# An expert layer's low weight parts move from VectorE to GpSimd, and accumulations are waited for by slot

## The reference

```python
xt = x.reshape(B * S, d)                                  # 4096 x 256
scores = jax.nn.softmax(xt @ router_w, axis=-1)
expert_weights, expert_idx = jax.lax.top_k(scores, 2)
h = gelu(jnp.einsum('td,edf->tef', xt, w1)) * jnp.einsum('td,edf->tef', xt, v1)   # F = 704
y = jnp.einsum('tef,efd->ted', h, w2)
yk = jnp.take_along_axis(y, expert_idx[:, :, None], axis=1)
out = jnp.sum(expert_weights[:, :, None] * yk, axis=1) + bias
```

## Time and profile before

| | before |
|---|---|
| time, median of 3 runs | 918.5 us (917.31 to 919.8) |
| the profiled execution's own time | 916.48 us |
| its span | 914.7 us |
| expert stage | from about 403 us to the end |
| PE busy | 823.5 us, 90% of the span |
| DVE busy | 578.7 us, 63% |
| POOL busy | 445.7 us, 49% |
| ACT busy | 370.3 us, 40% |

### The profile page before, as it was taken

How to read it: one execution, slowest core, us unless ns; L and a number is a source line. 1 busy time by engine, 2 the same in 40 slices (tenths; PEclk the granted TensorE clock), 3 DMA queues, 4 the chain that set the end, 5 groups by cost and what they waited for, 6 DMA issues and landing times.

```text
span 914.7 us, 19914 instructions
## 1 busy us (share of the span) xinstructions
PE 823.5 (90%) x5017; PEld 730.6 (80%) x5018; DVE 578.7 (63%) x1636; ACT 370.3 (40%) x672; POOL 445.7 (49%) x444
## 2 busy tenths in 40 slices
PE   6799999999999985019999999999999999999994
PEld 2588898898989874018998988989989898999993
DVE  6668777888758565504666565566665756655553
ACT  4775666657474332103233242342432434232221
POOL 1344655968668685822345344343343533433433
PEclk9799999999999986559999999999999999999998
DMA  7111050211302314362224224242252222222221
GB/s 266 36 47 47 2 167 24 94 63 55 93 3 94 95 34 147 128 219 55 46 35 132 47 35 132 45 132 36 38 141 35 35 43 39 35 39 42 35 47 17
DMA packets 49207, 65.31 MB, mean 71 GB/s; under 512 B 4944, under 2 KB 43984, under 8 KB 49168
## 3 DMA queue, kind: packets, MB, share of 16 engines
q1 hardware_dynamic: 35200, 46.03, 17.5%
q0 software_dynamic: 13392, 18.27, 9.9%
q10 hardware_dynamic: 576, 0.54, 0.2%
HBM read 41.28 MB, written 23.54 MB: 71 GB/s over the span
## 4 chain that ended last, share of the span: by engine, by line
PE 83%; POOL 5%; DMA 3%; DVE 3%; issue 2%; ACT 2%; SPq 1%; DVEq 0%; ACTq 0%; POOLq 0%
PE ps L1379 13%; PE ps L1381 13%; PE ps L1380 13%; PE ps L466 10%; PE ps L468 10%; PE ps L467 10%; PE ps L1412 5%; DMA out_rows<-y_moe,tok_moe 2%; POOL routed L1248 2%; PE ps L1388 2%; PE ps L558 1%; PE ps L1427 1%; PE ps L1426 1%; POOL w_moe_lo L371 1%; PE ps L515 1%
## 5 line engine op out<-in xcount | busy, mean ns | idle before, releaser
L1565 POOL TENSOR_TENSOR y_moe<-y_moe 128x256 f32<-128x256 f32 x71 | 51.9, 731 | 245.1 <-DVE y_moe L1529 245.1
L1379 PE MATMUL ps<-w_moe_hi,xT_moe_hi 128*128 x426 | 167.4, 393 | 1.4 <-DVE xT_moe_lo L1511 1.4
L1381 PE MATMUL ps<-w_moe_lo,xT_moe_hi 128*128 x426 | 161.4, 379 | 0.0
L1380 PE MATMUL ps<-w_moe_hi,xT_moe_lo 128*128 x426 | 161.1, 378 | 0.0
L1571 POOL DMA_INDIRECT out_rows<-y_moe,tok_moe x71 | 111.2, 1566 | 33.9 <-issue 33.4
L1470 ACT ACTIVATE hidT_hi<-ps 128x768 fp32r<-128x768 f32 x71 | 57.9, 815 | 163.8 <-PE ps L1412 163.8
L1464 ACT ACTIVATE gelu_moe<-ps 128x704 f32<-128x704 f32 x71 | 54.0, 760 | 133.8 <-PE ps L1381 133.8
L1379 PE MATMUL ps<-w_moe_hi,hidT_hi 128*128 x355 | 105.8, 298 | 2.3 <-issue 2.3
L1381 PE MATMUL ps<-w_moe_lo,hidT_hi 128*128 x355 | 100.3, 283 | 0.0
L1380 PE MATMUL ps<-w_moe_hi,hidT_lo 128*128 x355 | 99.9, 281 | 0.0
L1529 DVE SCALAR_TENSOR_TENSOR y_moe<-ps,gate_moe,gates 128x256 f32<-128x256 f32 x142 | 62.1, 479 | 51.8 <-PE ps L1427 45.8
(11 more groups left out here) (195 smaller groups left out, 1973.5 us busy)
## 6 DMA issues: line engine op xcount, KB each, us to landing
raw<-in_w SPq DMA_DIRECT2D x8, 1408.0 KB
x_moe<-routed SPq DMA_DIRECT2D x74, 132.5 KB, 2.2
raw<-in_w SPq DMA_DIRECT2D x8, 640.0 KB
x_sb<-in_x SPq DMA_DIRECT2D x8, 512.0 KB, 3.7
x_again<-in_x SPq DMA_DIRECT2D x8, 512.0 KB
out_rows<-x_again SPq DMA_DIRECT2D x8, 512.0 KB
gu_raw<-in_gu_t SPq DMA_DIRECT2D x1, 1536.0 KB, 7.3
out_rows<-y_moe,tok_moe POOLq DMA_INDIRECT x71, 4.2
```

Of the source, the lines that this page charges most:

```text
L1379: pe.matmul(dst, a_hi, b_hi, start=first, stop=False)
L1380: pe.matmul(dst, a_lo, b_hi, start=False, stop=False)
L1381: return pe.matmul(dst, a_hi, b_lo, start=False, stop=last)
```

## The change

The low parts of the first layer's weights are made on POOL instead of DVE: at an expert change POOL makes three pieces in a row (128x1408 twice, 128x1536 once) ahead of the accumulation of the tile. DVE's step has no split and no table entry for it. The two waits for `added` on DVE are set by the four slots: in step t, `take_gates` of tile t+1 waits for tile t-3, and `gate_y` of tile t-1 for tile t-5. Seven tiles instead of three are written out ahead of the loop, since the loop's body may now only hold tiles with t >= 4 for these waits; SP's loads keep their distances.

```diff
--- before.py
+++ after.py
@@ -1316,7 +1316,7 @@
             def near(self, d):
                 return Tile(self.n + d, self.turn)
 
-        ALONE = 3
+        ALONE = 7
 
         def tiles(engine, first, step, last):
 
@@ -1365,11 +1365,13 @@
                 load_rows(Tile(n))
                 if n == 1:
                     load_weights(sp, 2, 3, 1)
+                if n >= SLOTS + 2:
+                    load_behind(Tile(n - SLOTS - 1))
 
             with sp.Fori(0, (MOE_TILES - ALONE) // SLOTS, 1) as turn:
                 for n in range(SLOTS):
                     load_rows(Tile(n + SLOTS + ALONE - 1, turn))
-                    load_behind(Tile(n + 1, turn))
+                    load_behind(Tile(n + ALONE - 2, turn))
             for n in range(SLOTS):
                 sp.wait_ge(rows_in[n], ((MOE_TILES + SLOTS - 2 - n) // SLOTS + 1) * 16)
 
@@ -1502,8 +1504,8 @@
                 v.tensor_tensor(g[:, 2:3], g[:, 0:1], g[:, 1:2], ALU.mult).then_inc(gate_steps, 1)
                 v.wait_ge(gate_steps, t.v * 2 + 2)
                 v.tensor_tensor(g[:, 3:4], g[:, 0:1], g[:, 2:3], ALU.subtract)
-                if t.n >= ALONE:
-                    v.wait_ge(added, (t.v - ALONE + 1) * 16)
+                if t.n >= SLOTS:
+                    v.wait_ge(added, (t.v - SLOTS + 1) * 16)
                 v.tensor_copy(tok_moe[:, t.slot, :], tok).then_inc(gates_r, 1)
 
             def xT_rest(t):
@@ -1523,8 +1525,8 @@
             def gate_y(t):
                 v.wait_ge(y_mm, t.v + 1)
                 v.wait_ge(gates_r, t.v + 1)
-                if t.n >= 2:
-                    v.wait_ge(added, (t.v - 1) * 16)
+                if t.n >= SLOTS:
+                    v.wait_ge(added, (t.v - SLOTS + 1) * 16)
                 for b in range(B):
                     i = v.scalar_tensor_tensor(y_moe[:, t.slot, b, :], y_ps[t.par], gate_moe[:, t.slot, 3 - b:4 - b],
                                                gates[:, b, 1, :], ALU.mult, ALU.mult)
@@ -1547,18 +1549,21 @@
                 take_gates(t.near(1))
 
             def step(t):
-                e = to_be_split(v, t)
                 multiply(t)
                 xT_rest(t.near(1))
                 gate_y(t.near(-1))
                 hidT_rest(t)
                 take_gates(t.near(1))
-                split_behind(v, e, t, split_w13_lo)
 
             tiles(v, first, step, gate_y)
 
         @block.gpsimd
         def _(g):
+            def split_lo(g, e, buf, t):
+                g.wait_ge(we_hi, 3)
+                split_w13_lo(g, e, buf)
+                split_w2_lo(g, e, buf)
+
             def add_rows(t):
 
                 g.wait_ge(y_r, t.v + 1)
@@ -1574,7 +1579,7 @@
 
             def step(t):
                 e = to_be_split(g, t)
-                split_behind(g, e, t, split_w2_lo)
+                split_behind(g, e, t, split_lo)
                 add_rows(t)
 
             tiles(g, add_rows, step, lambda t: None)
```

## The result

The changed kernel takes 943.66 us (median of 4 runs, 942.32 to 946.25) against 919.15 for the kernel before in the same series: a ratio of 1.027, with an interval of 1.025 to 1.029. The change makes the kernel slower by 24.5 us. The direction was forecast, the size was not: the forecast was 922.7 with 918 to 928 around it. The profiled execution after took 943.01 us and spans 941.2; before, it was 916.48 and 914.7.

A forecast was written before the change was run, and what follows sets the result against it. PE bounds the kernel, with gaps worth 9.3 us, mostly waits for DVE's `hid_moe` at six expert changes. Gaps of 13.5 after against 9.3 give +4.2: 920.6 on the profiled 916.5, 922.7 on the median 918.5; range 918 to 928.

The forecast's parts named there:

- The price of the split on DVE: PE's gap at each of six expert changes, 1.41 us, goes with line 361 off DVE; with the wider waits about 9 us.
- Nothing for the waits, the loop and the removed table entry: Seven tiles ahead of the loop cost nothing; DVE's removed table entry gains nothing; wider waits remove only the small remaining gaps.
- POOL's pieces: Three queued pieces on POOL at each change, 3.2 us each; the accumulation begins 3.6 later, hidden with some 1.1 us to spare.
- Operations with both inputs in SBUF stop: In DVE's take_gates, lines 1502 and 1504 are blocked while POOL subtracts, until the POOL instruction has finished.
- Who gets in between two POOL instructions?: Line 1502 runs between POOL's second and third piece; 1504 waits until 490.8 or 490.9, making PE's gap 2.0 one step later.
- POOL keeps the ports: Rival: DVE's 1502 waits until POOL's pieces end, 1504 behind the sum too: gap 2.7 at six changes, 927; chance 0.18.
- The margin at the first change: At the first expert change line 1504 of step t, expected about 480.1, precedes POOL's first piece, expected at 480.9.
- the other case: Clause within a rival of chance 0.18: first piece queued by 479.9 stops line 1504 of step t; gap 2.7, 927.
- The sum: PE's gaps after: 6 x 2.0 + 1.4 + 0.3 less 0.2, 13.5; before 9.3; net +4.2.
- The first rival: One-column operations get through, or POOL leaves 0.2 us between second and third piece: every gap goes, 909.4; chance 0.14.

The follow-up runs named there:

- the half change: Wider waits and seven tiles ahead of the loop, split left on DVE, against the kernel before: 918.21 against 918.86, ratio 0.9997.
- the experiment with both reductions: Kernel before plus two unused sums over a constant tile (1024 and 512 columns) behind DVE's split at each change: 937.62 against 917.72, ratio 1.0218.

## Why the prediction was right and wrong, by its steps

**The price of the split on DVE: right.** The removal was put at about 9 us. With the block avoided the excess over quiet steps falls from 9.3 to 0.0.

**Nothing for the waits, the loop and the removed table entry: right.** Shown by the half change (0.9997).

**POOL's pieces: right.** They start 3.2 us apart (554.51, then 6.96 us for two with the overlap, third at 560.87), and are queued; the accumulations stay hidden: the cast never waits for one, and `gate_y` is no later for them than in a quiet step.

**Operations with both inputs in SBUF stop: right, and shown.** The Trainium skill (SBUF — State Buffer, "Who interferes with whom") says the second to start is blocked until the first has finished. The runs agree as to the block and its strictness, down to one column. They add to "finished": at the pieces of this kernel it is the whole run of queued POOL instructions, 4.97 and 10.48 us here, not the one instruction inside which DVE asked.

**"Who gets in between two POOL instructions?": the step that failed.** I took it that DVE's waiting operation is let in between two of POOL's, from one place at 295, where POOL's line 1224 took 0.38 instead of 0.19. The place was read rightly. The timeline of DVE in the kernel before has the operation by itself:

```profile
295.19 1.54 DVE L1007 SCALAR_TENSOR_TENSOR rows<-x_again,mv,mod 128x256 f32<-128x256 f32 x1
```

It takes 0.48 in the median; here it stood from 295.19, through POOL's line 1214 (until 296.44), and ended at 296.73, ahead of POOL's line 1224 (296.79). What failed was to carry this one handover over to the pieces: at none of the handovers from piece to piece, or from the last piece to the sum, was a waiting operation let in at the changed kernel's six changes. The place with the opposite answer was in hand, at 161, where POOL's sum passed an operation that DVE had already asked for the earlier trace rows; it went to the rival *POOL keeps the ports* with 0.18. That rival is what happened: five gaps of 2.73 to 3.48, sum 14.7, where I took 2.0 to 2.3 for each. What makes the place at 295 different is not shown. One difference is on record: POOL's records overlap by 0.03 us there and by 0.5 to 0.6 at the pieces.

**The margin at the first change: failed.** I expected POOL's first piece about 1 us behind line 1504 of the same step, and named the other case in a clause. The last of the two operations came 0.27 us later behind the first than in other steps (482.21 where 481.94 was due), POOL's piece started at 482.40, and the operation was held through three pieces: a gap of 8.5 in place of 2.0. The gaps together are 23.2 against the forecast 13.5. On time the operation would have stood 0.46 ahead of the piece, as at the second change, where it passed. The same lateness (0.22 to 0.27 us, once in the stage) stands at the first change of all four kernels that have both the pieces on POOL and seven tiles ahead of the loop. It is absent with either half alone: with the pieces on DVE and seven tiles ahead, and with the pieces on POOL, the old waits and three tiles ahead. Its cause is open.

**A term that was missing: TensorE's clock.** The sum priced a gap as its length. The steps behind the gaps cost 8.7 us more, and the tail, where the idle time at the loop's exit is the same as before, 1.8. With my own gap of 2.0 the term would have been nothing (none of six behind gaps of 1.9 to 2.0). Over all profiles of this document, a gap of up to 2.1 us at an expert change never had the lowered clock behind it, and behind 25 of the 28 gaps of 2.5 us and more in the steps the next step was longer. So the first error called up the second. The Trainium skill (TensorE: Matmul & The Clock Gate, "Part 1") says the gate halves TensorE's clock after idle time, and that its looking isn't tied to the program's own steps; the windows agree with the half (0.50), and the gap of 2.83 with only 0.06 behind it, where the three others of 2.73 to 2.82 have 1.3 to 1.7, would fit the second. No run here shows what decides in a single case.

**The first rival: wrong as drawn, right in its other condition.** One column doesn't get through by being narrow. But a pause between POOL's pieces does let both operations through, as it said: with 0.27 us of pause the kernel takes 912.66. Whether 0.2 would do was not tried.

Together: the gaps 9.7 us above the forecast, the clock 8.7, the late start 2.0 and the tail 1.8 are 22.2 of the 22.4 us between the forecast for the profiled execution (920.6) and its 943.0. The rival *POOL keeps the ports*, at 927, had the mechanism and nearly the gap (2.7), but neither the first change nor the clock.

## What to carry to other kernels

When elementwise work moves to GpSimd, list every VectorE instruction that may fall into it with two tensor inputs in SBUF, however small, and price each, as the bad case, as blocked until GpSimd's queue runs dry, not until the current instruction ends. Two remedies cost nearly nothing here: the small operations in the form with a scalar operand (911.7), or a wait of GpSimd for its own result between long instructions (912.7, with gaps left at one change). And price an idle gap of TensorE on the bounding path as its length plus what the lowered clock takes behind it, unless a row shows that a gap of this length leaves the clock alone.

## What was not expected of the hardware

- POOL's queued pieces hold DVE off as one: DVE's operation of one column took 4.97 and 10.48 us with recorded overlaps of 0.5 to 0.6 us between POOL's, and 1.22 us with pauses of 0.27. It isn't so at every pair of POOL instructions: at 296.4 in the kernel before, with an overlap of 0.03, DVE's waiting operation came first.
- An operation with one tensor and a scalar operand isn't blocked though the scalar's column lies in SBUF too: 72 of 72 at 0.21 to 0.22 us, those inside POOL's pieces among them. The compare and the copy of one column just ahead weren't held inside POOL's pieces either (0.15 and 0.14 us at 560.39 and 560.46 in the changed kernel).
- A block can begin earlier than POOL's record: the first piece is recorded from 0.5 us before the end of the indirect DMA ahead of it, and an operation recorded 0.18 to 0.19 us before the piece was held by it in three kernels. At 0.40 us and more ahead none was.
- The clock's price isn't the same for the same gap: 0.06 to 1.7 us behind gaps of 2.73 to 3.48, 2.7 behind the one of 8.5; in the experiment with both reductions nothing to 2.8 us behind gaps of 3.0 to 3.1.
